# The second half of each attention step issued two steps late instead of one

## The reference

```python
xn = _layernorm(x)                        # x: 8 x 2048 x 1024, f32
q, k = rotary(xn @ Wq.T), rotary(xn @ Wk.T)    # 16 heads of 64
v = xn @ Wv.T
scores = einsum('bhqd,bhkd->bhqk', q, k) * 64**-0.5, causal
attn = softmax(scores)
out = einsum('bhqk,bhkd->bhqd', attn, v) @ Wo.T
ffn = sum over 8 experts: (silu(xn W1) * (xn W2)) W3 * gate     # top 2 gates non-zero, all 8 computed
return x + out + ffn
```

## Time and profile before

| what | us |
|---|---|
| median of 2 runs (5954.62 and 6701.64) | 6328.13 |
| the profiled execution | 5957.63 |
| its span on the slowest core | 5956.0 |
| spans of all eight cores | 5945.6 to 5956.0 |
| the eight attention stages and the projections between them | 414.79 to 2121.48 |

### The profile page before, as it was taken

How to read it: one execution, slowest core, us unless ns; L and a number is a source line. 1 busy time by engine, 2 the same in 40 slices (tenths; PEclk the granted TensorE clock), 3 DMA queues, 4 the chain that set the end, 5 groups by cost and what they waited for, 6 DMA issues and landing times.

```text
span 5956.0 us, 72483 instructions; the slowest of 8 cores (5945.6 to 5956.0 us)
## 1 busy us (share of the span) xinstructions
PE 5007.4 (84%) x24880; PEld 2454.9 (41%) x24880; DVE 2524.5 (42%) x4628; ACT 993.3 (17%) x2017; POOL 282.4 (5%) x536
## 2 busy tenths in 40 slices
PE   3345666666566569999999999999999999999998
PEld 2333333333334334444444444444444444444444
DVE  3346556656655633333333333333333333333333
ACT  2223222222322301001011011011011010110110
POOL 0000000000000000000000000000000000000000
PEclk8565665565566579999999999999999999999999
DMA  1010000000000012222222222222222222222222
GB/s 42 18 23 1 10 10 1 10 10 1 10 10 1 3 20 37 40 41 37 36 35 38 40 36 38 38 38 39 38 37 40 41 37 36 35 46 34 36 41 80
DMA packets 81885, 173.71 MB, mean 29 GB/s; under 512 B 9336, under 2 KB 9592, under 8 KB 81536
## 3 DMA queue, kind: packets, MB, share of 16 engines
q0 software_dynamic: 76496, 152.13, 16.7%
q1 hardware_dynamic: 5040, 16.94, 0.8%
HBM read 312.74 MB, written 8.39 MB: 54 GB/s over the span
## 4 chain that ended last, share of the span: by engine, by line
PE 79%; DVE 13%; issue 4%; ACT 3%; DMA 1%; DVEq 0%; ACTq 0%; SPq 0%; POOLq 0%
PE pp L610 21%; PE pp L620 20%; PE pp L655 20%; DVE stat L460 6%; DVE poolb L414 4%; PE pp L423 4%; PE pp L452 4%; PE pp L336 4%; PE pp L542 1%; PE pp L405 1%; PE pp L380 1%; PE pp L259 1%; ACT poolb L473 1%; ACT poolb L479 1%; PE pp L246 1%
## 5 line engine op out<-in xcount | busy, mean ns | idle before, releaser
L610 PE MATMUL pp<-xn,poolb 128*128 128x512 bf16 x5632 | 1341.2, 381 | 0.4 <-ACT arf L630 0.4
L620 PE MATMUL pp<-xn,poolb 128*128 128x512 bf16 x5632 | 1334.7, 380 | 0.0
L655 PE MATMUL pp<-poolb 128*128 128x512 bf16 x5632 | 1218.7, 379 | 0.0
L634 DVE TENSOR_TENSOR arf<-pp,arf 128x512 f32<-128x512 f32 x704 | 487.1, 692 | 1442.5 <-PE pp L620 1442.5
L630 ACT ACTIVATE arf<-pp 128x512 f32<-128x512 f32 x704 | 420.8, 598 | 2619.2 <-PE pp L610 2619.2
L610 PEld LDWEIGHTS pp<-xn,poolb 128*128 128x128 bf16 x5632 | 552.4, 98 | 671.8 <-issue 13.9
L620 PEld LDWEIGHTS pp<-xn,poolb 128*128 128x128 bf16 x5632 | 552.6, 98 | 669.7 <-issue 9.4
L655 PEld LDWEIGHTS pp<-poolb 128*128 128x128 bf16 x5632 | 551.1, 98 | 663.8
L665 DVE TENSOR_TENSOR acc<-acc,pp 128x512 f32<-128x512 f32 x512 | 352.3, 688 | 845.4 <-PE pp L655 845.4
L405 PE MATMUL pp<-dgb,poolb 128*128 128x128 bf16 x2176 | 305.8, 304 | 340.9 <-DVE poolb L414 268.7
L640 DVE TENSOR_TENSOR poolb<-arf 128x512 bf16<-128x512 f32 x704 | 487.7, 693 | 74.9 <-DVE arf L634 2.3
(11 more groups left out here) (81 smaller groups left out, 1638.8 us busy)
## 6 DMA issues: line engine op xcount, KB each, us to landing
poolb<-w_l POOLq DMA_DIRECT2D x352, 256.0 KB, 4.2
poolb<-w_l POOLq DMA_DIRECT2D x128, 352.0 KB, 4.4
arf<-x SPq DMA_DIRECT2D x16, 512.0 KB, 3.5
out<-arf SPq DMA_DIRECT2D x16, 512.0 KB, 2.7
poolb<-wq_l POOLq DMA_DIRECT2D x8, 256.0 KB, 3.8
poolb<-wqs_l POOLq DMA_DIRECT2D x8, 256.0 KB, 5.5
poolb<-wk_l POOLq DMA_DIRECT2D x8, 256.0 KB, 5.1
poolb<-wks_l POOLq DMA_DIRECT2D x8, 256.0 KB, 4.6
```

The lines of the kernel that those rows point to most:

```text
L610: em("tensor", [(lambda cc, tt, bk, kkc, fi, la: lambda e: e.matmul(pps(BK(bk)), pb[:, W1B[cc % 2] + kkc * 128:W1B[cc % 2] + (kkc + 1) * 128],
L620: em("tensor", [(lambda cc, tt, bk, kkc, fi, la: lambda e: e.matmul(pps(BK(bk)), pb[:, W2B[cc % 2] + kkc * 128:W2B[cc % 2] + (kkc + 1) * 128],
L634: em("vector", (lambda bk, tbb, ebb, tt: lambda e: e.tensor_tensor(arfs(H2S[tbb], 512), pps(BK(bk)), arfs(WBC[ebb] + tt * 512, 512), ALU.m ...
L655: em("tensor", [(lambda mm, tt, bk, cll, fi, la: lambda e: e.matmul(pps(BK(bk)), pb[:, W3B[mm % 2] + cll * 128:W3B[mm % 2] + (cll + 1) * 128],
```

## The change

`s2_stage` is now called with a depth of two: in unit u for unit u-2, and the call stands ahead of exp(u) instead of behind L479. Two stages are left over after unit 31. The two buffers of the probabilities and of `dgb` stay two; unit u-2 and unit u have the same `py`, so exp(u) overwrites what T(u-2) reads. No instruction is added or taken away.

```diff
-            prev = None
+            pipe = []
             for qb in range(NB):
                 for a in range(2):
...
                        writes=[("arf", DIAG + py * 128, DIAG + py * 128 + 128)])
+                    if len(pipe) >= 2:
+                        s2_stage(*pipe.pop(0))
+                    pipe.append((qb, a, py))
                     if qb > 0:
                         em("scalar", (lambda qq, b0, s0, pr: lambda e: e.activation(
...
-                    if prev is not None:
-                        s2_stage(*prev)
-                    prev = (qb, a, py)
                     if qb > 0:
                         em("vector", (lambda s0: lambda e: e.tensor_tensor(
...
-            if prev is not None:
-                s2_stage(*prev)
-                prev = None
+            for st_ in pipe:
+                s2_stage(*st_)
+            pipe = []
```

## The result

The changed kernel is slower: 6188.11 us, median of eleven runs, against 5969.51 us for ten runs of the kernel before. The ratio is 1.037, with a 95% interval of 1.033 to 1.041; executions in which the cores of a die ran at a lower clock are left out of it. The profiled execution took 6186.8 us against 5957.6: 229 us more, where 239 were forecast.

The account below looks back on a forecast made before the run. Attention stages were taken as bound by a chain over several engines (small units: L460, exp, short operations), no engine full. Terms summed to 29.8 us per head pair, times 8 = 239, on 5957.6: 6196 us, 4.0% slower; range 6120 to 6270.

Parts of the forecast that it names:

- Rival 1: Even units stall too, exp(u) starting behind PV(u-2) or T's last bank being later: 6368 us in full; chance 0.06.
- rival 3: Small odd units cost nothing because their stall is taken up somewhere: 6123 us; chance 0.04.
- rival 2: Copy doesn't hold up exp; ACT works past it or PV is done before: 5906 to 5977 us; chance 0.06.
- (c): Copy L434 ahead of exp in odd units: exp waits for casts, PV, copy; 9.1 us small, 12.3 large per head pair.
- (a): T(u-2) on PE no longer waits for `dgb`: at most 71.2 us, taken as 0.
- (b): exp(u) overwrites the buffer T(u-2) reads and waits for its last T; taken as 0 for even units.
- (d): End of a head pair, two stages left over: 21.4 us from L460 of (15,1) instead of 13.0, 8.4 more.

Follow-up runs that it names:

- the first experiment: The changed kernel with the copy L434 issued behind exp(u) and the diagonal instead of ahead of them: 5978.3 us profiled, 5984.0 in one more run.
- third experiment: The kernel before with depth two at the old place and three buffers instead of two, so nothing is overwritten early: ratio 1.003, profiled execution 5978 us.

## Why the prediction was right in its mechanism, and the step that failed

**The mechanism, its place and its price** came out as forecast: the copy holds exp in the odd units alone, and 229 us were measured where 239 were worked out. Rival 1 (even units stall too) is refuted by the even periods, rival 3 (small units cost nothing) by (3,1), rival 2 (the copy doesn't hold up exp) by the first experiment. The chances of the three cases that are slower by more than 2% (0.84, 0.06, 0.04) add up to 0.94, where the prediction says 0.93.

**The step that failed is the base of the sum.** The prediction says "My sum is made against 5957.6 and says nothing of the other", and then gives the forecast as an absolute time, 5957.6 + 239 = 6196 us. The median shown for the kernel before was 6328.13 us, the midpoint of two runs 747 us apart. Beside it the number 6196 forecasts a kernel 2% faster, while the text says 4.0% slower: the time and the direction contradict each other, and the time had the wrong one. What the runs showed in place of that base is 5969.5 us, the median of ten, and 6188.1 after it: 1.037, slower. Against 5969.5 the forecast of 6196 is 1.038, against the profiled execution it was made from 1.040. That 6188 lies in the range of 6120 to 6270 holds only because the kernel before turned out near the lower of its two times, for which no row gave a reason; that part is luck. With such a base a forecast has to be given as a ratio, with the time that it is taken against.

**Term by term**, in us per head pair. The term that was sized worst is (c), 20.1 measured for 21.4:

| term | forecast | measured |
|---|---|---|
| (a) no wait for `dgb` | 0 | 0 (third experiment) |
| (b) exp waits for T | 0 | 0 (first against third experiment) |
| (c) small odd units | 9.1 | 8.4 |
| (c) large odd units | 12.3 | 11.7 |
| (d) end of the pair | 8.4 | 8.7 in the last; 8.6 as the mean over seven, with the projections behind it |
| sum | 29.8 | 28.6 (229 / 8) |

The measured halves of (c) are sums of the differences between the median periods of (1,1) to (7,1) and of (8,1) to (14,1). The size that was off is the hand-over from the copy to exp. I let exp begin when the copy ends, 0.27 us behind its start, and allowed only for more; in the timeline above the copy starts at 2030.03 and exp at 2030.19, 0.16 later, and so it is for 117 of the 120 exps behind a copy. In the other direction PE started S 0.14 behind the accumulator read (2031.83 to 2031.97), where I had allowed 0.1. That is 0.11 us less in each of 14 units and 0.04 more in seven, 1.26 us of the 1.3 by which (c) came out smaller. Term (b) is 0 with less to spare than I thought: exp(12,0) moved back by 1.58 us and not by 1.4, and 0.56 us were left before S (first experiment).

**Whether ACT holds a ready exp**, the prediction had left open. In (12,1) of the timeline above the maximum, the diagonal and T(11,1) were done at 2027.5 (2026.95 + 0.58), and exp started at 2030.19, behind the copy; with the copy moved behind it, in the first experiment, the period fell from 9.87 to 7.79 us. The Trainium skill's rule of a strict first-in first-out queue on ScalarE (TensorE: Matmul & The Clock Gate, section "Architectural detail: the array is 16× 32×32, not 1× 128×128") agrees with both.

## What to carry to other kernels

When a software pipeline gets deeper, list for each in-order engine what stands ahead of the instruction that the chain needs, and in which unit the inputs of that are now made. Here ACT's list did not change at all, and yet every second exp was held, because the matmuls behind a 0.27 us copy had moved by one unit. And deepen only the part that lies on the chain: the whole second half two units late was worth nothing even without stalls (1.003; what it saved in the units it lost at the end of each pair), while PV alone two units late was worth 4%.

## What the runs showed that I had not expected

- ACT starts an instruction 0.16 us behind the start of a copy that takes 0.27 by its row; this holds for 117 of the 120 exps behind a copy in the changed kernel, so neighbours on ACT overlap in this trace.
- The largest waits need not cost anything: in the first experiment exp waits 520.0 us in all for T, twice as long as in the changed kernel, in a kernel that is 208 us faster.
- The granted clock at the end of a head pair rises at different points in kernels that differ only in order (0.55 then 1.00 in one, 0.50 then 0.83 in the other), and the time from the last L460 of a pair to the next pair's first varies from pair to pair of one execution by up to 2.9 us (47.3 to 50.2 in the kernel before). The two shortest of the seven are those in which the clock rises 9 us behind the last L460. An estimate for such a seam has that much play.
